# A two-layer graph kernel on one core: layer 1's gather ring goes from three rows and three PSUM sums to two and two, with a loop body a third as long, and layer 0's first one-hots are made earlier

## What is computed

```python
h = relu(layernorm(x))
# layer 0: for each of 8 heads
feat = h @ W[h];  logit = leaky_relu(feat@a1 [src] + feat@a2 [dst])
att  = softmax of logit over the edges of one src
x1 = x + relu(segment_sum(att * feat[dst], src))
h1 = relu(layernorm(x1))
# layer 1
agg  = segment_sum(batchnorm(h1)[src], dst) / degree
conv = relu(agg @ W_conv + b_conv)
out  = x1 + batchnorm(conv + attention(first 256 nodes of h1) + h1)
```

## Time and profile before

| what | value |
|---|---|
| median of 3 runs | 3770.28 us (3757.16 to 3771.27) |
| profiled execution's own time | 3779.02 us |
| its span, first to last instruction | 3777.2 us |
| mean granted TensorE clock | 0.839 |
| PE, DVE, ACT, POOL busy | 2698.9, 2523.8, 1012.0, 1896.5 us |

### The profile page before, as it was taken

How to read it: one execution, slowest core, us unless ns; L and a number is a source line. 1 busy time by engine, 2 the same in 40 slices (tenths; PEclk the granted TensorE clock), 3 DMA queues, 4 the chain that set the end, 5 groups by cost and what they waited for, 6 DMA issues and landing times. The chain is left out here.

```text
span 3777.2 us, 46121 instructions
## 1 busy us (share of the span) xinstructions
PE 2698.9 (71%) x10787; PEld 1629.9 (43%) x10788; DVE 2523.8 (67%) x4220; ACT 1012.0 (27%) x3108; POOL 1896.5 (50%) x1926
## 2 busy tenths in 40 slices
PE   1897457777777777777761587777777777778990
PEld 1554246665666556665551352322223232233440
DVE  9899956676666666666678655555555555555667
ACT  6543324443444444443432610000000000000220
POOL 0000055555555555555545236666566666564567
PEclk6898668998889898898885678888888888888995
DMA  4110266666666666666648436566566566564226
GB/s 161 43 44 35 58 183 176 190 187 184 179 184 184 182 183 184 189 188 181 186 131 300 159 89 173 169 172 172 167 175 175 169 171 173 166 172 145 92 67 233
DMA packets 235997, 601.79 MB, mean 159 GB/s; under 512 B 58488, under 2 KB 58488, under 8 KB 235952
## 3 DMA queue, kind: packets, MB, share of 16 engines
q0 software_dynamic: 136960, 456.11, 42.2%
q1 hardware_dynamic: 98992, 145.15, 11.9%
HBM read 547.02 MB, written 54.10 MB: 159 GB/s over the span
## 5 line engine op out<-in xcount | busy, mean ns | idle before, releaser
L491 POOL DMA_INDIRECT big<-feat_table,idx x880 | 840.9, 956 | 1084.2 <-issue 682.5
L1185 POOL DMA_INDIRECT big<-h_table,idx x832 | 786.5, 945 | 575.8 <-issue 341.5
L904 PE MATMUL psA<-big,onehot 128*128 128x260 f32 x1760 | 487.9, 425 | 108.6 <-DVE big L712 89.0
L904 PE MATMUL psB<-big,onehot 128*128 128x260 f32 x1760 | 491.3, 427 | 22.8 <-DVE acc L722 16.8
L904 PEld LDWEIGHTS psA<-big,onehot 128*128 128x128 f32 x1760 | 354.6, 209 | 192.9 <-issue 108.5
L540 ACT ACTIVATE big<-big,late_weights 128x65 f32<-128x65 f32 x1760 | 434.2, 341 | 0.0
L1640 PE MATMUL psCD<-big,onehot 128*128 128x512 f32 x554 | 355.3, 727 | 100.5 <-DVE acc L1433 51.3
L1640 PE MATMUL psA<-big,onehot 128*128 128x512 f32 x556 | 351.4, 717 | 99.2 <-DVE acc L1433 78.3
L1640 PE MATMUL psB<-big,onehot 128*128 128x512 f32 x554 | 353.6, 724 | 95.5 <-DVE acc L1433 73.4
L904 PEld LDWEIGHTS psB<-big,onehot 128*128 128x128 f32 x1760 | 356.2, 212 | 93.0 <-DVE acc L722 25.3
L514 ACT CAST idx<-minorB 128x8 int32 (+1 forms) x107 | 21.4, 203 | 1225.8 <-DMA big<-h_table,idx 1207.2
(11 more groups left out here) (366 smaller groups left out, 3780.2 us busy)
## 6 DMA issues: line engine op xcount, KB each, us to landing
nodes_all<-slot_nodes SPq DMA_DIRECT2D x112, 256.0 KB
big<-feat_table,idx POOLq DMA_INDIRECT x880
big<-h_table,idx POOLq DMA_INDIRECT x832
feat_table<-big SPq DMA_DIRECT2D x49, 264.0 KB, 2.1
x_table<-acc SPq DMA_DIRECT2D x49, 256.0 KB, 3.6
h_table<-big SPq DMA_DIRECT2D x49, 256.0 KB, 2.0
big<-h_table SPq DMA_DIRECT2D x49, 256.0 KB, 2.6
big<-x_table SPq DMA_DIRECT2D x49, 256.0 KB, 4.2
```

The costliest lines, as they stand in the source:

```text
L491: g.indirect_dma_start(ring[:, b.k, q * SB + u, :], None, feat_table, bass.IndirectOffsetOnAxis(ap=idx[:, 2 * b.k + q, u:u + 1], axis=0)). ...
L904: ins = pet.matmul(psum[:, 512 * hf:512 * hf + HALF_W], onehot[:, q, u % SB, :], ring[:, b.k, u, HALF_W * hf:HALF_W * (hf + 1)], start=(u ...
L1185: g.indirect_dma_start(rows_l1[LOTS * r.place + b // 2][:, b % 2 * D:(b % 2 + 1) * D], None, h1_table, bass.IndirectOffsetOnAxis(ap=idx[:, ...
```

## The change

Four edits. First, layer 1's ring has two rows and two PSUM sums, so that TensorE may start lot k when the add of lot k-2 is done, a gather may run 16 lots ahead of TensorE, not 24, and the loop body covers two rows (52 rounds, none left over). The gathers' wait for "aT" is gone with the third place. Second, `make_onehotT` for batch 0 stands ahead of the second `slot_fields`, whose node field goes to the second one-hot buffer (`withinB`), not to `wk2`. Third, TensorE does `look_up` of batch 0, then `turn_fields` of B, then `pass_batch(None, batch(0))`, and waits for `sortB_done` only after it. Fourth, `wait_rstd` stands three stages later, inside level 7 of `sort_both`.

```diff
-        LOT1_CREDIT, ADD1_CREDIT = 3 * SB, 3
+        LOT1_CREDIT, ADD1_CREDIT = 2 * SB, 2
...
-            for q in range(2):
-                make_onehotT(batch(0), q)
             pass_batch(None, batch(0))
...
             for q in range(2):
                 look_up(batch(0), q, load_tiles(pe, tileA, q))
+            turn_fields(sortB, 2)
             pass_batch(None, batch(0))
+            pe.wait_ge(sortB_done, 1)
...
-        rows_l1 = row_bufs((rows_flat, 4), (ad_flat[:, 6 * D:], 4), (rows2_flat, 2), (wk_flat, 2))
+        rows_l1 = row_bufs((rows_flat, 4), (ad_flat[:, 6 * D:], 4))
         RING1 = len(rows_l1) // LOTS
-        CYCLE = 2 * RING1
-        assert RING1 == 3
+        CYCLE = RING1
+        assert RING1 == 2
...
-            return (psA, psB, psC)[(r.c * SB + b) % 3]
+            return (psA, psB)[b % 2]
...
-                if r.i is None and r.c == RING1 - 1:
-                    SPE.wait(pool, "aT")
...
-                    pe.wait_ge(lot1_added, r(SB, b + ADD1_CREDIT - 2))
+                    pe.wait_ge(lot1_added, r(SB, b + ADD1_CREDIT - 1))
...
             sort_both(1, 6)
+            sort_both(7, 7, 0, 3)
             wait_rstd()
-            sort_both(7, ROW_BITS - 1)
+            sort_both(7, 7, 3, 7)
+            sort_both(8, ROW_BITS - 1)
...
             kB, other = sorted_keys_of(sortB)
-            slot_fields(kB, other, minorB, nodeB, tileB, 2, False)
+            for q in range(2):
+                dve.wait_ge(row_loaded[q], 16)
+                v.tensor_scalar(onehotT[q], nodes_all[:, q, :], iota_col[:, 0:1], None, ALU.is_equal).then_inc(onehotT_ready, 1)
+            slot_fields(kB, other, minorB, nodeB, tileB, 2, False, withinB)
             v.memset(small[:, 4:5], 0.0).then_inc(sortB_done, 1)
...
-            turn_fields(sortB, 2)
-            pe.wait_ge(sortB_done, 1)
-            layer0_tensor(pe)
+            layer0_tensor(pe, turn_fields)
```

More of the change, by code:

```diff
@@ L121, in build @@
         tileB = tables[0:1, 1, :, :].rearrange("p a r -> p (a r)").bitcast(I16).rearrange("p (r b) -> p r b", b=SB)
+        withinB = onehot[:, 1, :, :].rearrange("p b n -> p (b n)")
         tile_of_chunk = nodes_all[0:1, :, :].rearrange("p q c -> p (q c)").bitcast(I32).rearrange("p (r b) -> p r b", b=SB)
@@ L846, in layer0_vector, with layer0_tensor @@
             layer1_vector(dve, link, links)
-        def layer0_tensor(pe):
+        def layer0_tensor(pe, turn_fields):
             def look_up(b, q, tiles):
@@ L1044, in turn @@
                 n = self.c // RING1
-                return n * per + plus if self.i is None else self.i * (2 * per) + (n * per + plus)
+                return n * per + plus if self.i is None else self.i * per + (n * per + plus)
             def ahead(self, n):
@@ L1063, in build @@
         idx3 = sem("idx3")
-        h_arrived = [[sem(f"h_arrived{q}{u}") for u in range(2)] for q in range(3)]
+        h_arrived = [[sem(f"h_arrived{q}{u}") for u in range(2)] for q in range(RING1)]
         onehot1_ready = sem("onehot1_ready")
@@ L1980, in sort_rows, with sort_both @@
                     flip(srt, ROW_BITS + 1)
-            def sort_both(first, last):
+            def sort_both(first, last, begin=0, end=ROW_BITS):
                 for m in range(first, last + 1):
-                    for j in range(m - 1, -1, -1):
+                    for j in list(range(m - 1, -1, -1))[begin:end]:
                         dve.wait_ge(sortA.step, sortA.steps)
@@ L2018, in wait_rstd, with slot_fields @@
                 v.tensor_tensor(stat[:, 1, :], stat[:, 1, :], stat[:, 3, :], ALU.mult).then_inc(rstd_ready, 1)
-            def slot_fields(sorted_keys, other, minor_t, node_t, tile_t, turns, first):
+            def slot_fields(sorted_keys, other, minor_t, node_t, tile_t, turns, first, within):
                 bits = sorted_keys.bitcast(I32)
@@ L2031, in slot_fields @@
                 link(v.tensor_scalar(seg, seg, P - 1, None, ALU.bitwise_and))
-                link(v.tensor_tensor(wk2, other, seg, ALU.add))
+                link(v.tensor_tensor(within, other, seg, ALU.add))
                 if first:
                     dve.wait_ge(Wa_ready, 1)
-                    v.tensor_copy(oh_flat.bitcast(BF16)[:, 0:COLS], wk2).then_inc(fields, 1)
+                    v.tensor_copy(oh_flat.bitcast(BF16)[:, 0:COLS], within).then_inc(fields, 1)
                     link(v.tensor_tensor(joined[:, 1:COLS], segment[:, 1:COLS], segment[:, 0:COLS - 1], ALU.is_equal))
@@ L2097, in _ @@
             kA, other = sorted_keys_of(sortA)
-            slot_fields(kA, other, minorA, None, tileA, 1, True)
+            slot_fields(kA, other, minorA, None, tileA, 1, True, wk2)
             v.memset(small[:, 2:3], 0.0).then_inc(slotsA, 1)
@@ L2196, in turn_fields @@
                 pe.wait_ge(fields, turn)
-                for source, target in ((srt.bufs[:, srt.last_at, :], psA), (wk2, psB)):
+                for source, target in ((srt.bufs[:, srt.last_at, :], psA), (wk2 if turn == 1 else withinB, psB)):
                     for b in range(SB):
```

## The result

The changed kernel takes 3853.62 us (median of 4 runs, 3850.02 to 3868.63) beside 3766.2 us for the kernel before: a ratio of 1.0257, 95% interval 1.0232 to 1.0283. The profiled execution took 3851.75 us, its span is 3849.9.

The account below looks back on a forecast made before the run. Layer 1's loop was taken as bound by GpSimd's gathers, 10.0 us a row, plus 218 us lost in episodes of late TensorE signals. Terms 66 + 0 + 5 - 2 - 5 = +64 on 3770.3 gave 3834 us, range 3725 to 3900.

Parts of the forecast that it names:

- Three sums become two: Layer 1's loop: one finished lot fewer in PSUM per late-signal episode, 51 x 1.3 = +66 us, bounds 0 and +103.
- some 51 episodes still: Sign in layer 1's loop: the periods of late TensorE signals, with 4 us nameless waits, keep their number.
- The rate between episodes: Layer 1's loop: two sums allow up to 9.0 us a row, below GpSimd's 10.0; priced at nothing, +52 at most.
- Three ring rows become two: Layer 1's loop: gathers 16 lots ahead instead of 24 still suffice, cost 0; uncovered, up to 10.0 us a row.
- Loop body of two rows: Layer 1's loop: 51 jumps back instead of 16, 0.26 us each on VectorE; +5 us, between 0 and 9.
- `wait_rstd`: VectorE's 8.48 us stall for ScalarE's variances shrinks to 1.3, most moving to crossing A0; -2 us, bounds -1.7 and -7.2.
- Layer 0's start: One-hots ahead of the second unpacking remove VectorE's 4.86 us wait for a load; -5 us, bounds 0 and -15.8.
- may shrink or stay: Layer 0's 7.24 and 3.66 us waits for TensorE's signals amid gathers, said to be late next.
- the episodes don't care: Rival, layer 1's loop: gathers alone set the late signals, so the third sum was worth nothing; 3768 us, chance 0.20.
- code fetched for the long body: Rival, layer 1's loop: late waits are instruction fetches and vanish, wholly 3545 us, a quarter 3709; shared chance 0.18.
- The costlier rival: Layer 1's loop: the third sum was worth more, GpSimd's slack being of no use; +162, 3932 us, chance 0.10.
- The rule of the Trainium skill: Cycling through PSUM banks leaves TensorE idle spells, swings its clock and lowers throughput; by it two sums would only gain.

Follow-up runs that it names:

- Experiment 1: Kernel before with two PSUM sums instead of three in layer 1's loop, nothing else changed: 3847.26 us, ratio 1.022.
- experiment 3: Changed kernel with a layer 1 loop body of six rows instead of two: 3844.39 us, ratio 1.0206 to the kernel before.
- experiment 8: The whole changed kernel measured again, in a group without late signals: 3213.36 us beside 3201.7 for the kernel before, ratio 1.0034.
- experiment 5: Changed kernel with layer 1's loop as before, leaving only the front parts (`wait_rstd` later, layer 0's start): 3201.09 us beside 3202.32, ratio 0.9991.
- experiments 6: Kernel before with every other gather of layer 1's loop left out, one run: 3038.48 us, loop 855.7 us.
- 7: Kernel before with layer 1's gathers a quarter as wide, their number kept, one run: 3206.27 us, loop 1019.4 us.
- experiment 10: Kernel before with two ring rows and a 1 us GpSimd memset ahead of each row's gathers: 3300.05 us, ratio 1.0308.
- 11: Kernel before with every other gather of layer 1's loop left out, run once more in another group: 3038.42 us, loop 855.8 us.
- experiment 12: Kernel before with four PSUM sums, node numbers read from SBUF, `wait_rstd` later and layer 0's new start: 3240.58 us beside 3203.5, ratio 1.0119.

## Why the prediction came out as it did

**The loss came where it was foretold and near the size foretold, but its main term is made up otherwise.** 3834 was the forecast, 3853.6 is the result; 64 us were to be lost and 87 were; the loop was to take 1329 us and took 1340.

*Three sums become two*, +66. Experiment 1, in which nothing else is changed, shows that the sums carry the loss, and the traces show what was to be its source: behind each late lot one finished lot instead of two. The working of the term, 51 x 1.3, is not shown. It took the number of episodes as fixed ("some 51 episodes still") and made each of them longer by most of a lot. Counted by the late adds there are 59 and 61, and the seven steps of one take 14.66 and 14.20 us beside 14.52 before. By this count most of the loss is eight to ten more episodes, 55 us in experiment 1 and 69 in the changed kernel, where an episode 0.3 us shorter gives 20 back. That 66 comes so near is partly luck. With four sums there are 48 episodes, with three 51 and 54, with two 57 to 61; why fewer sums bring more of them stays open.

*The rate between episodes*, priced at nothing with 52 us kept for the upper end: this term was mis-sized. The steps outside of the episodes take 1.16 us in experiment 1 and 1.17 in the changed kernel instead of 1.09, which is 27 and 32 us (21 and 37 by the other count). The reasoning was that GpSimd's 10.0 us a row hide a row of 9.0. They do in the later groups, where 1.7 us are left. In the first group GpSimd stops in the episodes for want of free buffers; that VectorE then catches up at its own rate between two of them, and a slower rate is paid for there, is argued from this and was not tried by itself. The shortest row without a late add takes 7.76 us before and 8.73 after; 8.2 and 9.0 were worked out.

*Three ring rows become two*, 0: confirmed in the first group (1257.8 and 1258.2). Where no signal is late it costs 9.9 us once. The prediction had named "up to the 10.0 us of its gathers", for each row, if there were no cover; it is the third row's eight gathers alone, which then stand in the loop. That the cover in the first group was the time lost in episodes is argued.

*Loop body of two rows*, +5: neither shown nor refuted. Three kernels with two sums have loops from 1326.5 to 1348.7 us and don't order by it; in the later groups it and the two sums come to 1.7 us together.

*`wait_rstd`*, -2: 0.85 us of idle are left (1.3 foretold) and 5.53 stand before the first instruction of A0 (some 5 foretold). The stall moved as described.

*Layer 0's start*, -5: together with the last the first add of layer 0 comes 7.2 us earlier, 7 foretold. Whether they arrive at the end wasn't measured in the first group, where the front parts alone didn't run. The two waits that "may shrink or stay" became a single one of 12.87 us.

**The rivals.** That the episodes don't care fell by experiment 1. That code fetched for the long body causes the late waits fell by experiment 3 and by the changed kernel itself: with bodies of two and of six rows there are 61 and 57 episodes, and none of the long bodies in the later groups has any. The costlier rival (3932) was too dear by 78 us, though its second term was partly real. The rule of the Trainium skill that was cited against the forecast (TensorE: Matmul & The Clock Gate, section on psum-queue depth-cycling) isn't borne out by these traces: in experiment 8 TensorE cycles through two sums at a granted clock of 1.00.

**What stays open** is why TensorE's signals are late in one group of runs and never in three others, with the clock at 0.84 and 1.00. In the trace of the kernel before GpSimd had gathered without a break for 6.0 to 10.7 us when the first late lot ended, in all 51 episodes, and in 50 of them the last late add starts 1.8 us (median; 0.3 to 3.0) after GpSimd has stopped gathering. In the changed kernel five of the 61 episodes begin within 3 us behind a pause of the gathers, so it is no firm rule, and experiment 5 has 1010 us of gathers in a row and no late signal. That the gathers have to do with it is argued from the timelines only: the four runs that should have tested it (experiments 6, 7, 10 and 11) came where there were none. The lower clock is not what makes signals late in experiment 10, where TensorE falls to the lower level after standing still and every signal is on time; in the first group the clock's fall is likewise seen after TensorE has stood still, but what else belongs to the cause there isn't shown.

**No version was shown to beat both kernels everywhere.** Four sums gain 20 us in the first group; with the front parts they lose 37 in the fourth. The kernel before with the front parts alone is no slower in the second group, the only one where it was measured.

## What to carry to other kernels

A buffer between two engines is worth most when its source falls silent, so count the silences; but don't take their number as fixed when a buffer goes: here it rose from 51 to 59 and 61, and that was most of the cost. Count them by the signal itself (the end of the work against the start of what waits for it) and not by a bar on idle time, and see whether the count holds when the bar moves. A rate that is hidden behind a slower engine is hidden only while that engine sets the time. And measure a change beside the kernel before in each group of runs: here the same edit costs 2.6% in one and 0.3% in another, from different terms.

## What the runs showed of the hardware that was not expected

The same program takes 3764 us in one group of runs and 3202 in three others, with a spread of 0.8% at most in each; nearly all of the 562 us between them lies in the two stages that gather (layer 0's loop 1440 and 1120 us, layer 1's 1258 and 1022). A gather of 128 rows takes GpSimd 0.95 us and 0.30 of issue whether it brings 512 or 128 values a row. Where a one-hot matrix is built from two operands in SBUF, a gather that starts meanwhile takes 1.31 us on average instead of 0.95 (100 of 102 in experiment 12); with one operand in PSUM it keeps its 0.95 (all 102 in experiment 5). And TensorE's fall to the lower level of its clock needs no late signal: in experiment 10 it came after 2.12 us of waiting for a gather.
